# A float32 linear-attention decoder: the high parts of W1 rounded by ScalarE instead of GpSimd, the low parts in two pairs

## What is computed

```python
for i in range(8):                          # B = 8 layers, H = 16 heads, K = 64, F = 1024
    residual = x
    Q  = elu(x @ Wq[i] + bq[i]) + 1
    Kf = elu(x @ Wk[i] + bk[i]) + 1
    V  = x @ Wv[i] + bv[i]
    KV, sumK = sum(Kf * V, tokens), sum(Kf, tokens)
    att = Q * KV / (Q * sumK + 1e-6)
    x = layer_norm(gelu(att @ Wo[i] + bo[i]) + residual, ln1)
    residual = x
    h = gelu(x @ W1[i] + b1[i])             # W1 is 256 x 1024
    x = layer_norm(gelu(h @ W2[i] + b2[i]) + residual, ln2)
```

## Time and profile before

| | us |
|---|---|
| runs shown: 3002.4, 3004.3, 3007.04, median | 3004.3 |
| the profiled execution | 3003.99 |
| its span, first to last instruction | 3002.3 |
| TensorE matmul busy | 2851.9 (95%) |
| VectorE busy | 2353.7 (78%) |
| ScalarE busy | 1867.5 (62%) |
| GpSimd busy | 777.2 (26%) |

### The profile page before, as it was taken

The page is one execution under the profiler, slowest core; times in us unless marked ns, Lnnn a source line. Parts: engine busy times, 40 slices in busy tenths (PEclk is TensorE's granted clock), DMA queues, the critical chain, the costliest instruction groups (busy, mean ns, idle before and its releaser), DMA issues. The chain is left out here.

```text
span 3002.3 us, 37724 instructions
## 1 busy us (share of the span) xinstructions
PE 2851.9 (95%) x12878; PEld 2307.5 (77%) x12879; DVE 2353.7 (78%) x3523; ACT 1867.5 (62%) x2797; POOL 777.2 (26%) x514
## 2 busy tenths in 40 slices
PE   5899999999999999999999999999999986996999
PEld 4688888788878887888788878887888875775555
DVE  7878898889888988898889888988898836773111
ACT  5667777777777777777777777677767733441122
POOL 4003231323132313231323132313231124332122
PEclk8899999999999999999999999999999998996999
DMA  4000000000000000100000000000100016000121
GB/s 139 1 1 27 31 19 21 28 31 18 22 28 31 18 22 28 31 18 22 28 31 18 22 28 31 18 22 28 31 18 6 1 56 232 0 0 4 47 46 30
DMA packets 62501, 92.35 MB, mean 31 GB/s; under 512 B 16480, under 2 KB 42336, under 8 KB 60256
## 3 DMA queue, kind: packets, MB, share of 16 engines
q1 hardware_dynamic: 58224, 85.55, 9.0%
q0 software_dynamic: 4080, 4.34, 0.8%
HBM read 80.24 MB, written 10.54 MB: 30 GB/s over the span
## 5 line engine op out<-in xcount | busy, mean ns | idle before, releaser
L407 PE MATMUL PS<-XTHI,WHI 128*128 128x512 f32 x1536 | 624.7, 407 | 32.7 <-DVE EX L733 19.7
L409 PE MATMUL PS<-XTHI,WLO 128*128 128x512 f32 x1536 | 606.9, 395 | 0.0
L408 PE MATMUL PS<-XTLO,WHI 128*128 128x512 f32 x1536 | 602.9, 393 | 0.0
L618 ACT ACTIVATE ATT<-INV,CC,CE 128x128 f32<-128x128 f32 x1024 | 432.4, 485 | 124.1 <-PE Y L449 117.9
L449 PE MATMUL Y<-WO,ATT 128*128 128x256 f32 x2048 | 455.9, 381 | 5.8 <-ACT ATT L618 5.8
L449 PE MATMUL Y<-W2S,H 128*128 128x256 f32 x2048 | 457.5, 379 | 2.3 <-DVE T L805 1.4
L449 PEld LDWEIGHTS Y<-WO,ATT 128*128 128x128 f32 x2048 | 390.7, 191 | 62.7 <-ACT ATT L618 5.3
L449 PEld LDWEIGHTS Y<-W2S,H 128*128 128x128 f32 x2048 | 386.2, 190 | 56.3 <-DVE T L805 1.8
L407 PEld LDWEIGHTS PS<-XTHI,WHI 128*128 128x128 f32 x1536 | 291.0, 189 | 100.3 <-issue 32.5
L323 POOL TENSOR_TENSOR RSTD<-MV,EPS 128x4 f32<-128x4 f32 x68 | 16.1, 237 | 1357.2 <-DVE MV L820 1348.7
L583 ACT ACTIVATE EX<-PS,BNEG 128x512 f32<-128x512 f32 x256 | 165.7, 685 | 299.9 <-DVE INV L785 158.1
(11 more groups left out here) (187 smaller groups left out, 4679.9 us busy)
## 6 DMA issues: line engine op xcount, KB each, us to landing
STAGE<-L_attn_Wkvq SPq DMA_DIRECT2D x64, 384.0 KB, 3.1
WO<-L_attn_Wo SPq DMA_DIRECT2D x8, 1024.0 KB, 4.8
W2S<-L_attn_W SPq DMA_DIRECT2D x8, 1024.0 KB, 5.1
STAGE<-L_attn_W SPq DMA_DIRECT2D x32, 256.0 KB, 4.9
WGU<-L_ffn_r_gate SPq DMA_DIRECT2D x8, 512.0 KB, 9.3
WGU<-L_ffn_r_up SPq DMA_DIRECT2D x8, 512.0 KB, 9.1
WD<-L_ffn_r_down SPq DMA_DIRECT2D x8, 512.0 KB, 9.2
rows_in<-ZERO SPq DMA_DIRECT2D x1, 3128.0 KB, 16.0
```

Of the source, the lines that this page charges most:

```text
L407: nc.tensor.matmul(out, whi[:, kc, :], xhi[:, kc, :], start=(kc == 0), stop=False)
L408: nc.tensor.matmul(out, whi[:, kc, :], xlo[:, kc, :], start=False, stop=False)
L409: ins = nc.tensor.matmul(out, wlo[:, kc, :], xhi[:, kc, :], start=False, stop=(kc == KD - 1))
L618: ins = nc.scalar.activation(ATT[:, 2 * p + i, ss], INV[:, b, i, ss], ACT.Identity, scale=CE[:, b, k:k + 1], bias=CC[:, b, k:k + 1])
```

## The change

ScalarE now rounds W1's pieces too: a new `high_hidden` on ScalarE copies a piece from `STAGE` into `W1HI` and counts `w1_hi`. GpSimd's `split_hidden` becomes `low_hidden`: it waits for `w1_hi` and subtracts; its multiplication by one is gone. In the loop's step 4, ScalarE rounds pieces 8 and 9 before the keys of pair 1 and pieces 10 and 11 after the inversion of pair 1, ahead of the keys of pair 3. GpSimd subtracts for pieces 8 and 9 where all four stood before, and for pieces 10 and 11 after the reciprocal square root of the first norm. For layer 0, ScalarE rounds all four pieces in slot(0, 0), after the GELU of the Wo product; GpSimd's four subtractions stay ahead of its slot(0, 0).

```diff
-            def split_hidden(layer, k, first):
-
-                s, m = k % RING, 2 * (k - HC)
-                pool.wait_ge(staged[s], staged_value(layer, k))
+            def low_hidden(layer, k):
+
+                m = 2 * (k - HC)
+                pool.wait_ge(w1_hi, layer * (PIECES - HC) + (k - HC + 1))
                 hi, lo = (w[:, m:m + 2, :, :].rearrange("p m c n -> p (m c n)") for w in (W1HI, W1LO))
-                if not first:
-                    pool.wait_ge(h_mm, layer * TILES * HC + (m + 2 - HC))
-                src = STAGE[:, s, 0:2 * KD * P]
-                nc.gpsimd.tensor_tensor(hi, src, ONE[:, :].to_broadcast(src.shape), ALU.mult).then_inc(w1_hi, 1)
-                pool.wait_ge(w1_hi, layer * (PIECES - HC) + (k - HC + 1))
-                nc.gpsimd.tensor_tensor(lo, src, hi.bitcast(F32), ALU.subtract).then_inc(w_lo, 1)
+                nc.gpsimd.tensor_tensor(lo, STAGE[:, k % RING, 0:2 * KD * P], hi.bitcast(F32), ALU.subtract).then_inc(w_lo, 1)
@@ GpSimd's slot
                 if load and t == TILES:
-                    for k in range(HC, PIECES):
-                        split_hidden(l + 1, k, False)
+                    for k in range(HC, HC + 2):
+                        low_hidden(l + 1, k)
                 if tile:
                     rstd(RSTD[:, 0, :], MV[:, 0, :, 1], EPS1, mv1, 2 * g + 2, r1, g + 1)
...
+                    if load and t == TILES:
+                        for k in range(HC + 2, PIECES):
+                            low_hidden(l + 1, k)
                     r = R[:, t % 2, :, :]
                     pool.wait_ge(n1, g + 1)
@@ GpSimd, ahead of slot(0, 0)
             for k in range(HC, PIECES):
-                split_hidden(0, k, True)
+                low_hidden(0, k)
@@ ScalarE
+            def high_hidden(layer, ks):
+
+                for k in ks:
+                    m = 2 * (k - HC)
+                    act.wait_ge(staged[k % RING], staged_value(layer, k))
+                    if not (type(layer) is int and layer == 0):
+                        act.wait_ge(h_mm, layer * TILES * HC + (m + 2 - HC))
+                    nc.scalar.copy(W1HI[:, m:m + 2, :, :].rearrange("p m c n -> p (m c n)"),
+                                   STAGE[:, k % RING, 0:2 * KD * P]).then_inc(w1_hi, 1)
@@ ScalarE's slot
                 if load and t == TILES - 1:
                     high_parts(l + 1, range(6, HC))
+                if load and t == TILES:
+                    high_hidden(l + 1, range(HC, HC + 2))
                 if more:
                     clip_keys(nl, nt, 1)
...
                     gelu_down(y_b, y_act, g + 1)
                 if first:
                     high_parts(0, range(6, HC))
+                if type(l) is int and g == 0:
+                    high_hidden(0, range(HC, PIECES))
                 if more:
...
                     if load and t == TILES - 2:
                         high_parts(l + 1, range(2, 4))
+                    if load and t == TILES:
+                        high_hidden(l + 1, range(HC + 2, PIECES))
                     clip_keys(nl, nt, 3)
```

More of the change, by code:

```diff
@@ L188, in attention_stack @@
             sem(n) for n in ("k_mm", "v_mm", "q_mm", "y_mm", "x1t_mm", "h_mm", "z_mm", "xt_mm"))
-        w_hi, b_neg, clipped, ex, log, inv, y_act, x1_hi, h_act, z_act, xt_hi = (
-            sem(n) for n in ("w_hi", "b_neg", "clipped", "ex", "log", "inv", "y_act", "x1_hi", "h_act", "z_act", "xt_hi"))
+        w_hi, w1_hi, b_neg, clipped, ex, log, inv, y_act, x1_hi, h_act, z_act, xt_hi = (
+            sem(n) for n in ("w_hi", "w1_hi", "b_neg", "clipped", "ex", "log", "inv", "y_act", "x1_hi", "h_act", "z_act", "xt_hi"))
         snap, kf, wq, kv_mul, sums, stat, denom, residue, recip, xt_lo, x1_lo = (
@@ L196, in attention_stack @@
             sem(n) for n in ("y_b", "res1", "mv1", "x0", "n1", "z_b", "res2", "mv2", "n2", "mv0"))
-        half_set, w1_hi, w_lo, r1, r2, xn_s, xn, r0 = (
-            sem(n) for n in ("half_set", "w1_hi", "w_lo", "r1", "r2", "xn_s", "xn", "r0"))
+        half_set, w_lo, r1, r2, xn_s, xn, r0 = (
+            sem(n) for n in ("half_set", "w_lo", "r1", "r2", "xn_s", "xn", "r0"))
         att, att_s, x1, x1_s = (sem(n) for n in ("att", "att_s", "x1", "x1_s"))
```

## The result

| | before | after |
|---|---|---|
| median of 15 runs each, us | 3005.3 (3002.4 to 3008.15) | 3012.8 (3008.93 to 3015.2) |
| ratio, 95% interval | | 1.0026 [1.0019, 1.0033] |
| profiled execution, us | 3003.99 | 3013.81 |
| its span, us | 3002.3 | 3012.1 |

The changed kernel is slower by 0.26%, 7.5 us between the medians.

The account below looks back on a forecast made before the run. TensorE, busy 95%, was taken as the bound, with VectorE's chain in step 4 under 0.1 us from delaying it. The sum was 3003.99 - 4.9 (start) + 6.0 (stall) + 7.7 (loop) = 3012.8 us; 8-in-10 range 3001.5 to 3019.

Parts of the forecast that it names:

- signs: Expected timeline marks, among them L781 or L785 at 2.4 us in step 4 and 0.8 to 1.1 us idle before L527.
- 1, casts in the loop: ScalarE's four added casts per layer in step 4 fit its idle gaps and cost nothing, 0.63 us each.
- 2, multiplication gone, in the loop: GpSimd drops four multiplications per layer; VectorE's L769 gets back 0.9 us, but the loop gains nothing.
- Part 3: Loop step 4: low parts 10 and 11 hold VectorE's L781 or L785, costing 1.1 us per layer, 7.7 us.
- Part 4: First layer, about 47 to 58 us: VectorE freed from GpSimd's W1 splitting, a gain of 4.9 us.
- Part 5: slot(0, 0): ScalarE waits for piece 11's load with the exponential queued behind, a loss of 6.0 us.
- 6, queues: SyncE's later loads and W1's matmuls, which wait for the low parts, keep enough cover: no cost.
- faster: Rival: VectorE freed at 48 to 58 us keeps TensorE's clock up, gain 6.7 us, no losses: 2997.3 us; chance 0.10.
- two places in the loop: TensorE idles 1.6 us at the loop's branch and 1.42 us at L527's transposes in step 2.
- The low parts miss L781: Rival: in step 4 the two low parts avoid VectorE's L781, so the loop costs nothing: 3005.1 us; chance 0.16.
- the stall is hidden: Rival: in the first tile piece 11 lands sooner or slack covers ScalarE's wait: 3006.8 us; chance 0.10.
- As in step 2: Rival: in step 4 both L781 and L785 are held, 1.9 us per layer: 3018.6 us; chance 0.12.

Follow-up runs that it names:

- e6: The changed kernel with two more useless ScalarE copies of 512 columns behind the casts of pieces 10 and 11 in step 4: 3010.92 us, 1.0029.
- e4: The changed kernel with the edits of e2 and e3 together: 3001.99 us, 0.9991 of the kernel before.
- After_again: The changed kernel, unaltered, run again on another chip: 3011.75 us against 3003.36 for the kernel before, 1.0027.
- e7: The changed kernel with one more useless GpSimd subtraction between low parts 10 and 11 in step 4: 3018.18 us, 1.0047 of the kernel before.
- e2: The changed kernel with layer 0's cast of piece 11 moved behind the inversion of pair 1: 3008.34 us, 1.0009 of the kernel before.
- e3: The changed kernel with step 4's casts of pieces 10 and 11 ahead of pair 0's weighting, all four low parts ahead of the power: 3007.14 us, 1.0007.
- e10: The changed kernel with e4's edits, step 2's pieces 2 and 3 split earlier, and pieces 4 and 5 moved to step 3: 2980.55 us, 0.9928.

## Why the prediction was right, and where its sizes were off

The forecast, 3012.8 us, equals the measured median, and the mechanisms of its parts are in the profile. That it agrees to the tenth is luck. It added 8.8 us to 3003.99, where the medians lie 7.5 apart, and it started 1.3 us under the median of the kernel before, 3005.3; the two errors cancel. Nor were all signs met in size: L795 at 2.12 us (2.4 named), VectorE 0.90 us late (1.2), TensorE's idle time in step 4 at 0.70 us (0.8 to 1.1), and 0.87 us a layer lies just under the forecast's own 0.9 to 1.3. Its sizes, by its own parts:

| part | predicted, us | measured, us |
|---|---|---|
| 1, casts in the loop | 0 (0.63 each) | 0; 0.62 alone, 1.13 a pair; e6 |
| 2, multiplication gone, in the loop | 0 | 0; 0.93 + 0.84 on VectorE, not passed on |
| 3, two low parts behind the power | +7.7 (1.1 a layer) | +6.1 (0.87 a layer) |
| 4, start relief | -4.9 | -4.2 (-4.2 to -5.0 over eleven traces, mean -4.6) |
| 5, stall in slot(0, 0) | +6.0 | +5.75 |
| 6, queues | 0 | 0; no TensorE wait on GpSimd in the eight layers |

**Part 3, mechanism right, size off by a fifth.** The step that was missized is the hold of 1.2 us; it was 0.90. Measured from the start of the second inversion, as the prediction did, L795 is ready after 3.16 us, exactly as read in the earlier trace rows, and the low parts are done after 4.20 instead of 4.32; that is 0.1. Rounding took 0.05. The rest, 0.14, was in rows that I had: a held instruction doesn't begin from nothing. L795 ends 432.95, 1.08 us after GpSimd's 431.87, not 1.22. The rows of before show the same: L769 ends at 438.94, GpSimd's L373 at 437.86, 1.08 again, which I had read as "1.2". The scaling from VectorE's loss to TensorE's was taken as 1.78/1.93 = 0.92 and was 0.96 here, 0.86 of 0.90; the difference of 0.04 us fits the slack that the prediction put under 0.1.

**Part 4, mechanism right, one term unseen.** TensorE's gap fell from 6.60 to 1.66 us, 4.94, as worked out. But the relief that reached the end was 4.2 us in this profile. The exponential that VectorE waits for ended 10.83 us after TensorE's start at 42.99, before it was 10.09 after 41.50, 0.74 more. The cause is TensorE's clock behind the gap before: the matmuls took 0.63 us (granted clock 0.50, 1.2 GHz) instead of 0.39 (1.00, 2.4 GHz) up to 47.8 in the profile after, up to 44.6 in that of before. In e4 this phase was as short as before, and the interval 11.77 us, 5.0 less. After_again, the same kernel as after, takes 12.31, and e7, with the same start, 11.77. So up to 0.8 us of this term changes from execution to execution, with nothing in the kernel for it.

**The rival "faster" named a mechanism that happened and gave nothing.** It said that a gap of 1.7 us would leave the clock up. It does. Stretches of four us behind the gap, before and after: the stretch and its length, busy time and count of PE, PEld, DVE, ACT and POOL, then the granted clock, the share of the DMA engines and GB/s.

```profile
58.00:62.00 4.00, 3.74 (x9) 2.99 (x10) 3.93 (x7) 0.00 (x0) 0.39 (x1) 0.50 0.33 102
```

```profile
55.50:59.50 4.00, 3.95 (x17) 3.30 (x18) 3.93 (x6) 0.35 (x1) 0.00 (x0) 1.00 0.00 0
```

Before, nine matmuls in four us at a granted clock of 0.50; after, seventeen at 1.00. But VectorE (busy 3.93 of 4 us in both) is the bound of that stretch, and TensorE's gain went whole into its next wait:

```profile
72.31 1.94 PE L441 MATMUL PS<-ident,X 128*128 128x128 f32 x8 [3.76 <-DVE EX L733]
```

```profile
69.59 1.97 PE L439 MATMUL PS<-ident,X 128*128 128x128 f32 x8 [5.33 <-DVE EX L747]
```

From 58.26 to 72.31 it is 14.05 us, from 55.55 to 69.59 it is 14.04. The argument that stood against this rival, that VectorE is late next, was the right one.

**Part 5, right for the reasons given.** ScalarE's idle time was 3.58 us (3 to 4 expected), and the table load begins 5.76 us behind the GELU's end (6.0). The prediction's last cast took 0.8 us of its sum, where its own figure for a cast is 0.63; with that it comes to 5.9. e2 split the term into a wait and its late cast (4.2) and the three casts in front of the exponential (1.6); the prediction had them in one chain, and so had the right sum without having said that a third of it would stay if the wait went.

**The other rivals.** "The low parts miss L781" and "the stall is hidden" are refuted by the 0.70 and 10.43 us in the rows after; e3 and e2 show what each would have given. "As in step 2" was not what the change did, with 37.32 - 36.38 = 0.94 us a layer between the two: e7 needed a third subtraction for it. Which of the two comes about hangs on whether the waiting VectorE instruction finds one or two GpSimd instructions unfinished: one at 430.83 in the changed kernel, two at 577.59 in step 2 and at 428.13 in e7.

**A gap in the list of idle places.** The prediction named two places in the loop where TensorE stands still. The trace of before also has 0.37 us at the `X1LO` products and 0.24 behind them in step 2 of every pass. No term hung on them, but they were the way to the 7.7 us of e10.

On the rule of the Trainium skill, page "SBUF — State Buffer", section "SBUF: two separate sides" (one lock, for whole instructions): the runs agree with it, 0.90 us for a GpSimd pair that had 1.04 us to run, and turns taken instruction by instruction in e7. Whether a GpSimd instruction that only writes holds VectorE too was not tried.

## What to carry to other kernels

When one engine's chain has no slack to the bound engine for a stretch, list the instructions on it that share something with a helper engine, and place the helper's work by the clock, in a stretch with slack: here the same two subtractions a layer cost nothing in one place and 6 us in another, and clearing the two such places that step 2 of the kernel before already had gave about 20 of the 21 us (some 1 of them by taking ScalarE's casts out of the way of another), while the change of engine itself gave 1 to 3 at the most, not told from nothing by the times. Count what an edit takes off an engine only where that engine is late; and when a first-layer version of a loop edit waits for a load that its own output must free, look at what is queued behind the wait.

## What the runs showed of the hardware

- In these traces the hold between GpSimd and VectorE doesn't depend on the size of the VectorE instruction. In slot(0, 0) of the changed kernel two VectorE instructions on 128x8 elements, which take 0.15 and 0.17 us elsewhere, took 1.26 and 1.19 us beside the low parts:

```profile
115.06 1.26 DVE L786 SCALAR_TENSOR_TENSOR CC<-SUMS,ES 128x8 f32<-128x8 f32 x1
116.35 1.19 DVE L789 TENSOR_TENSOR CE<-CC,ES 128x8 f32<-128x8 f32 x1
```

- The two engines take turns: with several GpSimd instructions in a row and a VectorE one waiting, VectorE gets in after the current one, and then GpSimd waits (2.27 instead of 1.28 us in e7). In these traces no VectorE instruction lost more than about one GpSimd instruction (at most 2.0 us, beside L373 of 2.36).
- Not every VectorE instruction is held. Beside GpSimd, a TENSOR_SCALAR of 128x1024 with one tensor input took 1.56 us instead of 0.68 (e3) and the four L893 4.80 instead of 1.37; those that read PSUM kept their 1.41 a pair (L739 at 576.26) and the TENSOR_REDUCE its 2.29 (L756 at 399.19), both before.
- A held VectorE instruction of 128x1024 ends 1.08 us after the releasing one, where it takes 1.22 alone: 0.14 us of it lies under the hold.
- Two ScalarE casts of 512 columns take 1.13 us as a pair and 0.62 alone, 0.51 for the second.
- Gaps of 1.66 us at the start and of 1.59 in the loop leave TensorE's granted clock at 1.00. Gaps from 3.7 to 10.6 us are followed by 0.50 (3.76 before the transposes at 72.31 of the kernel before, where it was 1.00 ahead of the gap). How long it stays there was 3.1 us in one profile and 4.8 in another behind nearly the same gap (6.73 and 6.59 us).
